# Two-layer attention network: both halves of layer 0's bias in one product for half of the keys, the two heads' maxima at the two ends of a unit, products of ones ahead of the first work

## What is computed

```python
# layer 0: all tokens see all tokens, with a relative bias per head
q, k, v = heads(x @ Wq + bq), heads(x @ Wk + bk), heads(x @ Wv + bv)
attn = q @ k.T / sqrt(64)
attn += rel_bias_h[:, :, :, :, None] + rel_bias_w[:, :, :, None, :]
out = softmax(attn) @ v
y = out @ Wp + bp
# layer 1: 7 x 7 neighbourhood attention, no bias, weights qkv_w and out_w
```

## Time and profile before

| | |
|---|---|
| time, median of 3 runs | 3215.44 us (3212.84 to 3217.96) |
| the profiled execution's own time | 3214.5 us |
| its span, first to last instruction | 3212.7 us |
| PE busy | 3144.4 us |
| DVE busy | 1703.3 us |
| ACT busy | 1225.6 us |
| POOL busy | 1084.7 us |

### The profile page before, as it was taken

One profiled execution on the slowest core, in us unless ns is written; L12 is line 12 of the kernel. 1 busy time (PEld: TensorE's weight loads), 2 busy tenths in 40 slices (PEclk: granted clock), 3 DMA queues, 4 the chain that ended last, 5 costly groups with the idle time before them and its releaser, 6 DMA issues.

```text
span 3212.7 us, 48955 instructions
## 1 busy us (share of the span) xinstructions
PE 3144.4 (98%) x20428; PEld 2349.5 (73%) x20428; DVE 1703.3 (53%) x1889; ACT 1225.6 (38%) x1397; POOL 1084.7 (34%) x618
## 2 busy tenths in 40 slices
PE   8999999999999999999999999999999999999999
PEld 6875658887787656888778766688777866668876
DVE  4447745446435774543734577444463457744434
ACT  2345542124234654213423465321342355532132
POOL 0037770025003786002400477600330057750042
PEclk9999999999999999999999999999999999999999
DMA  3211013114421101311432100221153111031113
GB/s 124 93 35 26 20 49 115 40 54 130 139 95 27 25 20 50 114 40 61 159 126 72 34 21 18 84 90 40 59 174 108 66 37 24 14 111 59 40 34 115
DMA packets 170520, 220.39 MB, mean 69 GB/s; under 512 B 113856, under 2 KB 126400, under 8 KB 170304
## 3 DMA queue, kind: packets, MB, share of 16 engines
q1 hardware_dynamic: 168768, 215.68, 21.4%
q10 hardware_dynamic: 1536, 1.57, 0.2%
HBM read 141.70 MB, written 50.33 MB: 60 GB/s over the span
## 4 chain that ended last, share of the span: by engine, by line
PE 89%; issue 4%; ACT 3%; POOL 2%; DVE 1%; DMA 0%; SPq 0%; ACTq 0%; POOLq 0%
PE score L1157 15%; PE score L1158 14%; PE score L1159 14%; PE lot L1314 13%; PE score L1279 10%; PE lot L1229 5%; PE lot L1232 3%; PE score L1286 3%; PE score L1292 2%; PE lot L1331 2%; POOL acc L568 2%; PE lot L1262 2%; ACT prob L748 1%; PE lot L1200 1%; PE lot L1157 1%
## 5 line engine op out<-in xcount | busy, mean ns | idle before, releaser
L568 POOL TENSOR_TENSOR acc<-acc,prob 128x1024 f32<-128x1024 f32 x288 | 712.9, 2475 | 208.1 <-ACT prob L748 180.9
L748 ACT ACTIVATE prob<-score 128x1024 f32<-128x1024 f32 (+3 forms) x576 | 517.6, 910 | 416.6 <-PE score L1292 292.6
L889 DVE TENSOR_REDUCE max_part<-lot 128x1 f32<-128x512 f32 x640 | 411.3, 685 | 156.3 <-PE lot L1232 156.3
L1157 PE MATMUL score<-a_hi,w_hi 128*128 128x512 f32 x1152 | 458.9, 398 | 12.9 <-DVE q_lo L1002 5.1
L1314 PE MATMUL lot<-prob,v 128*64 128x512 f32 (+4 forms) x2496 | 462.2, 513 | 5.3 <-ACT o_raw L647 3.7
L1158 PE MATMUL score<-a_lo,w_hi 128*128 128x512 f32 x1152 | 450.7, 391 | 0.0
L1159 PE MATMUL score<-a_hi,w_lo 128*128 128x512 f32 x1152 | 450.0, 391 | 0.0
L568 POOL TENSOR_TENSOR acc<-prob 128x1024 f32<-128x1024 f32 x48 | 120.1, 2502 | 833.6 <-ACT prob L748 833.6
L1157 PE MATMUL score<-w_hi,a_hi 128*128 128x256 f32 x1152 | 336.1, 292 | 0.0
L1314 PEld LDWEIGHTS lot<-prob,v 128*64 128x64 f32 x2496 | 165.6, 137 | 232.0 <-issue 193.0
L1158 PE MATMUL score<-w_lo,a_hi 128*128 128x256 f32 x1152 | 325.5, 283 | 0.0
(11 more groups left out here) (112 smaller groups left out, 5370.2 us busy)
## 6 DMA issues: line engine op xcount, KB each, us to landing
raw<-weights SPq DMA_DIRECT2D x96, 768.0 KB, 4.4
g_mem<-g SPq DMA_DIRECT2D x24, 1024.0 KB, 4.7
xin<-x_t SPq DMA_DIRECT2D x24, 512.0 KB, 6.4
xr<-x_t SPq DMA_DIRECT2D x24, 512.0 KB, 5.2
x_mem<-xr SPq DMA_DIRECT2D x24, 512.0 KB, 6.6
xr<-x_mem SPq DMA_DIRECT2D x24, 512.0 KB, 5.4
y_t<-xr SPq DMA_DIRECT2D x24, 512.0 KB, 6.9
recip<-recip SPq DMA_DIRECT2D x368, 32.0 KB, 1.9
```

What stands on the lines that cost most here:

```text
L568: nc.gpsimd.tensor_tensor(acc[:, :, a:b], with_, now, ALU.add).then_inc(added, 1)
L748: nc.scalar.activation(prob[:, ug % P_SLOTS, :, 0:b - a], score[:, u % 2, :, 0:b - a], ACT.Exp, scale=SCALE).then_inc(prob_ok, 1)
L889: nc.vector.reduce_max(max_part[:, t, part, h:h + 1], lot[:, (2 * n + h) % 3, :], AX.X)\
L1157: nc.tensor.matmul(out, w[0], a[0], start=first, stop=False)
```

## The change

In layer 0 the tokens of the normalised input are put in another order: the 16 left columns of the image first (all 32 rows), then the 16 right ones. Keys and values keep that order; the queries are put back in image order when q is copied from PSUM (ACT, and DVE in two instructions instead of one). `onehot` now differs between the layers, so it is loaded in each phase (512 KB) and cast by DVE at `j == 3`. A key tile is then 8 image rows by 16 columns, so it needs 16 rows of the row part (of which it uses 8) and 16 of the column part.

For the key tiles 4 to 7 (from unit 6 in pair 0 and unit 4 in the others, and from unit 12 in the second half) the passes with `b_hi` and `b_lo` become one pass: SP copies the needed 32 rows of both side by side into `packed[0]` or `packed[1]` (64 rows for each head; `pack`, 12 DMAs for each half of a pair, SBUF to SBUF), and `key_block` takes the place of `onehot`. `packed[0]` and `max_wide0` lie where weight chunk 10 was loaded early, so that chunk is loaded during the last pair.

The maxima ahead of a unit are no longer a block before the scores. Head 0's two products are issued beside head 1's first two score products and head 1's two beside head 0's last two, and DVE waits for each head by itself (`half_mm`).

At the program's start PE multiplies six times ones by ones (128x128 by 512, fp32), and the order of the first normalisation's steps on DVE and PE is changed.

```diff
+BLOCK = SIDE // 2
+PACKED_FROM = ([6, 12], [4, 12])
...
+    packed = [m.put("packed0", [128, 2, HALF], F32R, at=slot_at[0]),
+              m.put("packed1", [128, 2, HALF], F32R, at=one + 40 * KB)]
+    max_wide0 = m.put("max_wide0", [128, 4, 256], F32R, at=slot_at[0] + 8 * KB)
...
+                    sp.wait_ge(pack_in[1], packed_no(f, p - 3))
...
+            def pack(f, p, h):
+                s = SET_OF[0][p]
+                sp.wait_ge(b_lo_ok, f // 2 * PAIRS + p + 1)
+                if p:
+                    sp.wait_ge(score_ok, unit_no(f, p - 1, (h + 1) * QT - 1))
+                else:
+                    sp.wait_ge(v_mm, (f + 1) * VN)
+                cols = slice(h * HALF, (h + 1) * HALF)
+                to = packed[h][:, :, :].bitcast(F32)
+                for e, part in enumerate((b_hi[s], b_lo[s])):
+                    for head in range(2):
+                        a, b = 64 * head, 64 * head + BLOCK * e
+                        for n in range(2):
+                            rows = part[a + BLOCK * n:a + BLOCK * n + BLOCK, cols].bitcast(F32)
+                            sp.dma_start(to[b:b + BLOCK, n, :], rows).then_inc(pack_in[h], 16)
+                        columns = part[a + SIDE:a + SIDE + BLOCK, cols].bitcast(F32)
+                        sp.dma_start(to[b + SIDE:b + SIDE + BLOCK, :, :],
+                                     columns.unsqueeze(1).to_broadcast([BLOCK, 2, HALF]))\
+                            .then_inc(pack_in[h], 16)
+            def load_onehot(f):
+                sp.dma_start(onehot_raw[:, :], onehot_src[f % 2]).then_inc(onehot_in, 16)
...
-                weights(f, 10)
+                    weights(f, 10)
+                else:
+                    pack(f, 0, 0)
+                    pack(f, 0, 1)
...
+                        sp.wait_ge(pack_in[1], packed_no(f, LAST - 1))
                         weights(f, 9)
+                    if p:
+                        pack(f, p, 1)
+                    if p == LAST:
+                        sp.wait_ge(score_ok, unit_no(f, LAST, QT - 1))
+                        weights(f, 10)
                     spread(f, p, 0)
+                    if p < LAST:
+                        pack(f, p + 1, 0)
...
+                if f + 1 < PHASES:
+                    load_onehot(f + 1)
...
+                        if j < CT:
+                            dst, src = by_columns(dst), in_blocks(src)
...
-                src = xr[:, i, :] if f % 2 else xin[:, i, :]
-                nc.vector.tensor_scalar(xin[:, i, :], src, group_mv[:, i, 0:1],
+                if f % 2:
+                    dst, src = xin[:, i, :], xr[:, i, :]
+                else:
+                    dst, src = in_blocks(x_norm[:, i, :]), by_columns(xin[:, i, :])
...
+                    dve.wait_ge(half_mm, 2 * n + h + 1)
...
                 if i == 2:
                     aggregate(0, 0)
+                    group_means(0, 0)
                 if i == 3:
-                    group_means(0, 0)
+                    group_variances(0, 0)
+                if i == 4:
+                    norm(0, 0)
+                    norm(0, 1)
+                    input_lo(0, 0)
             aggregate(0, 1)
-            group_variances(0, 0)
-            norm(0, 0)
-            norm(0, 1)
-            input_lo(0, 0)
-            group_means(0, 1)
             norm(0, 2)
             input_lo(0, 1)
             input_lo(0, 2)
+            group_means(0, 1)
             group_variances(0, 1)
...
+                            views = [(dst[:, b], src[:, b], hi[:, b]) for b in range(2)]
+                        for dst, src, hi in views:
+                            last = nc.vector.scalar_tensor_tensor(dst, src, bqk[:, j:j + 1], hi, ALU.add,
+                                                                  ALU.subtract)
+                        last.then_inc(qk_lo_ok, 1)
...
+                    if j == 3:
+                        dve.wait_ge(onehot_in, 16 * (f + 1))
+                        nc.vector.tensor_copy(onehot[:, :], onehot_raw[:, :]).then_inc(onehot_ok, 1)
...
-            def head_maximum(f, n, sums_before):
+            def head_pass(f, n, h, e):
                 p, k = n // (2 * QT) + 1, n % (2 * QT)
-                n += f // 2 * LAST * 2 * QT
-                banks_free(sums_before)
+                no = 2 * (n + f // 2 * LAST * 2 * QT) + h
+                if e == 0:
+                    if h == 0:
+                        maximum_ready(f, p, k)
+                    if no > 2:
+                        pe.wait_ge(half_max_ok, no - 2)
+                last = maximum_pass(no % 3, f, p, k, h, e)
+                if e:
+                    last.then_inc(half_mm, 1)
+                    halves_issued[0] = no + 1
+            def head_maximum(f, n):
+                banks_free()
                 pe.wait_ge(max_ok, maxima_issued[0])
-                if n:
-                    pe.wait_ge(half_max_ok, 2 * n - 1)
-                maximum_product((2 * n % 3, (2 * n + 1) % 3), f, p, k)
-                halves_issued[0] = 2 * n + 2
+                for e in range(2):
+                    for h in range(2):
+                        head_pass(f, n, h, e)
...
-            def scores(f, p, u):
+            def scores(f, p, u, n=None):
                 layer, s, slot = f % 2, SET_OF[f % 2][p], u % 2
                 t, a, b = unit_at(layer, u)
                 keys = slice(t * 128, (t + 1) * 128)
                 ug = units_before(f, p) + u
+                half = u // QT
+                is_packed = layer == 0 and t >= QT // 2 and u >= PACKED_FROM[p > 0][half]
+                passes = 4 if layer or is_packed else 5
+                def score_pass(k, h):
+                    w = (k_hi, k_hi, k_lo, None, None)[k]
+                    x = (q_hi, q_lo, q_hi, b_hi[s], b_lo[s])[k]
+                    if k < 3:
+                        w, x = w[rows_of(h), p, keys], x[rows_of(h), p, a:b]
+                    elif is_packed:
+                        w, x = key_block[rows_of(h), t % 2, :], packed[half][rows_of(h), int(t % 4 < 2), :]
+                    else:
+                        w, x = onehot[rows_of(h), keys], x[rows_of(h), a:b]
+                    return nc.tensor.matmul(score[:, slot, h, 0:b - a], w, x,
+                                            start=(k == 0), stop=(k == passes - 1))
+                def bias_ready(k):
+                    if is_packed and u in PACKED_FROM[p > 0] and k == 3:
+                        pe.wait_ge(pack_in[half], packed_no(f, p))
+                    if u == 0 and k == 3:
+                        pe.wait_ge(shifted, pair_no(f, p))
+                        if layer == 0:
+                            pe.wait_ge(b_hi_ok, f // 2 * PAIRS + p + 1)
+                    if u == 0 and k == 4:
+                        pe.wait_ge(b_lo_ok, f // 2 * PAIRS + p + 1)
                 if p == 0 and u < 2:
                     pe.wait_ge(v_ok, (f + 1) * VN)
                 elif ug >= 2:
                     pe.wait_ge(prob_ok, ug - 1)
-                for k, (w, x) in enumerate(((k_hi, q_hi), (k_hi, q_lo), (k_lo, q_hi))):
-                    for h in range(2):
-                        nc.tensor.matmul(score[:, slot, h, 0:b - a], w[rows_of(h), p, keys],
-                                         x[rows_of(h), p, a:b], start=(k == 0), stop=False)
-                if u == 0:
-                    pe.wait_ge(shifted, pair_no(f, p))
-                    if layer == 0:
-                        pe.wait_ge(b_hi_ok, f // 2 * PAIRS + p + 1)
-                for h in range(2):
-                    last = nc.tensor.matmul(score[:, slot, h, 0:b - a], onehot[rows_of(h), keys],
-                                            b_hi[s][rows_of(h), a:b], start=False, stop=(layer == 1))
-                if layer == 0:
-                    if u == 0:
-                        pe.wait_ge(b_lo_ok, f // 2 * PAIRS + p + 1)
-                    for h in range(2):
-                        last = nc.tensor.matmul(score[:, slot, h, 0:b - a], onehot[rows_of(h), keys],
-                                                b_lo[s][rows_of(h), a:b], start=False, stop=True)
-                last.then_inc(score_ok, 1)
+                if n is None:
+                    for k in range(passes):
+                        bias_ready(k)
+                        for h in range(2):
+                            last = score_pass(k, h)
+                    last.then_inc(score_ok, 1)
+                    return
+                banks_free(int(u in (2, 10)))
+                pe.wait_ge(max_ok, maxima_issued[0])
+                for k in range(passes + 2):
+                    if k < 2:
+                        head_pass(f, n, 0, k)
+                    else:
+                        last = score_pass(k - 2, 0)
+                    if k == passes + 1:
+                        last.then_inc(score_ok, 1)
+                    if k < passes:
+                        bias_ready(k)
+                        score_pass(k, 1)
+                    else:
```

(17 more changed lines are left out.)

119 lines of the change are left out of this document (70 added, 49 removed).

## The result

The changed kernel takes 3188.18 us (median of 4 runs, 3184.02 to 3189.43), the kernel before in the same comparison 3214.14 us (4 runs, 3212.64 to 3217.96). The ratio is 0.9915, 95% interval 0.9903 to 0.9927: 26.0 us faster. The profiled execution of the changed kernel took 3189.31 us with a span of 3187.5.

The account below looks back on a forecast made before the run. PE was taken as the bound, busy 3144 of 3213 us. Gains of 25.8 + 1.9 (packing), 3 (maxima) and 2.5 (start), less 0.8 (small additions), made 32.4 us: 3182 from 3214.5, range 3168 to 3198.

Parts of the forecast that it names:

- the signs named: Included middle pair 42.6 to 42.8 us, last pair within 0.5 us of before, unit 13 waiting about 0.6 us for ACT.
- 28 slots a phase: Layer-0 attention: of 46 packed units a phase, 28 give back a 0.23 us PE slot, 25.8 us in all.
- DVE needs 1.29 of 1.38 us, so it keeps up: Packed units with a maximum: DVE's work for two heads fits the shortened unit, so PE is not held.
- The margin of less than 0.1 us: Packed units: ACT's exponential fits about 1.3 us into 1.38; missing by 0.1 us repeatedly would cost 6 us.
- (a) Units 12 and 13: Pairs 1 to 4: ACT's chain makes shorter units wait, so both slots are lost, 8 a phase.
- (c) The last pair: POOL's unbroken additions hold the sums; 8 slots a phase lost, 0.3 us kept.
- Of the 8.1 us I keep 3: PE's waits for DVE's row maxima, twice a phase in pair 0: 3 us gained, bounds 0 and 8.1.
- The copies: SP's copies to packed, covered by 5 us before the first packed unit in pairs after pair 0; cost nothing.
- The start: Program start: earlier normalising and products of ones gain 2.5 us, bounds -1 and 6.
- Rival 2: ACT or DVE bounds packed units, half the 112 slots go: gain about 15 us, 3199; chance 0.07 for 6 to 14.
- Rivals 3 and 4: 3: freed slots waited for elsewhere, 3210 to 3220, chance 0.05. 4: first-half copies land late, kernel slower, chance 0.06.
- rival 1: Gain over 45 us: ACT chain at units 12 and 13 gives way, all maxima waits go, start gives 6; chance 0.06.

Follow-up runs that it names:

- the five-pass kernel: Changed kernel with its copies, waits and order kept, but five passes in every unit of layer 0; 3209.24 us, ratio 0.9979.
- the block order: Changed kernel with a unit's maximum as one block of four products ahead of its scores, as before the change; 3191.55 us, ratio 0.9927.
- shorter maxima: Changed kernel with DVE reading 384 of 512 columns for each head's maximum of pairs 1 to 5, part of the maximum left out; 3183.05 us, ratio 0.9893.
- the second trace: Profiled execution of the unaltered changed kernel run once more, 3182.3 us without any stretch at half rate; median 3186.39 us, ratio 0.991.
- the added products: Changed kernel with first bias, onehot cast and layer-1 rounding moved later, plus four more products of ones behind the first shift averages; 3172.94 us, ratio 0.9867.
- the first trace: First profiled execution of the unaltered changed kernel, with three stretches at half rate; 3189.31 us, span 3187.5.
- the kernel with the later first bias: Changed kernel with ACT's first bias copy of pair p+2 behind the output copy at unit 12 instead of behind unit 10; 3183.55 us, ratio 0.9903.
- the later layer-1 rounding: Changed kernel with ACT rounding the weight chunk of layer 1's last pairs behind unit 7 instead of unit 6; 3179.84 us, ratio 0.9896.

## Why the prediction was right, and where it was off

The forecast was 3182, the median 3188.18, a gain of 26 us where the sum said 32.4, in the range and on the right side. An execution without a stretch at half rate took 3182.3, but the sum did not know of these. Of the signs named, these came: PE waits 1.00 us for POOL at the last pair's first sums, 0.62 for ACT at unit 13, 2.7 for the maxima in all, and the first projection stands at 19.39. A middle pair of 42.85 us and a last pair 0.7 us shorter lie just outside what was named. Step by step:

1. **"28 slots a phase ... 25.8 us, plus ... 1.9 us"**, 27.7 us for packing. Measured by the five-pass kernel, with packing added last: 21.1 (26.7 when it is added first, see the block order). This is the term that was mis-sized, and the sentence that failed is "DVE needs 1.29 of 1.38 us, so it keeps up". It keeps up on average, but not behind a reciprocal of 1.75 us: then it reads seven heads without a break at 0.67 us each, and the weight loads wait. With shorter maxima a middle pair gains 1.75 instead of 1.25. That the waits of the weight loads (7.0 us) come near the shortfall (6.6) is in part chance: in the second trace they are 5.7 with the same pairs. By the marks, of the 1.65 us that are short in a phase 1.0 is at units 2 to 5 of pairs 1 to 4, behind the reciprocals, 0.45 at the end of pair 0, 0.2 at units 14 and 15 of pair 4, where PE waits for ACT, and about 0.4 is spread over the other stretches; the last pair gives 0.4 back. So the failed sentence is shown to cost 4 of the 6.6 us, and up to 6 with the end of pair 0, where the weight loads wait for DVE too. The margin of less than 0.1 us that the prediction feared for was ACT's; that one held. PE's waits for `prob` rose by 5.7 us, over half of it at unit 13 (0.35 to 0.62), where it was expected.
2. **(a) Units 12 and 13.** Right: the wait of 0.35 us became 0.62, the groups behind unit 13 gain 0.00, and moving ACT's rounding gives 0.2 to 0.3 us of it back.
3. **(c) The last pair.** The bound was right (POOL, 1.00 us of wait at the first sums), the size too low: 0.69 us from the last group of pair 4's values on, instead of 0.3. It is packing alone. The prediction counted only what the second half's sums would let go.
4. **"Of the 8.1 us I keep 3"**, less 0.8 for the split of q's rest. Measured for all that is not packing, without packing beside it: 7.4 us in attention, 4.0 of it at the end of pair 0 and 0.2 at units 2 to 5 of each pair. The waits for maxima fell to 2.7, and to 1.8 in the second trace, so 5.4 to 6.3 us came back: the waits did not return at the next bank. By the block order, the new order of the maxima is worth only some 0.4 us a phase next to packing, all of it in pair 0.
5. **The copies: nothing.** Right; 4 us of cover instead of 5. There are 576 copies a run, not 288, which is the number for the first halves alone.
6. **The cast of onehot: nothing.** Wrong, 2.8 us. It stands on DVE ahead of `g` of pair 1 (q's products with the table of the relative bias), and PE waits 0.7 us at L1294. The prediction asked what covers the cast, not what stands behind it on DVE.
7. **The start: 2.5 us.** Measured 4.35 at the first mark and 0.7 lost to the cast on the way, so 5.1. The mechanism named, the group mean ahead of POOL's w_lo, is right. What was missed is that the ones decide whether it happens, because they halve the time of the 14 small products. The clock at the first projection was not what they changed: behind 5.83 us of idle PE ran at half rate, 0.43 us a product, and with the added products at the full rate it started no earlier. The Trainium skill (TensorE: Matmul & The Clock Gate, The two states you'll see) lets an idle PE fall back to half rate, and by that rule the prediction kept only 0 to 2 us; the trace agrees with the rule, and not with that consequence. The reading that the clock rose some 5 us after dense work began was made from 28.94 on and left out a row: PE had been at work since 23.40, with averages between the projections. Before the change:

```profile
26.10 2.98 PE L1169 MATMUL lot<-shift,group 128*128 128x1 f32 x14
```

   The ones ended at 8.69 all the same, near the 9 us forecast: a right result on an incomplete reading. How much of the 5.1 us is this execution's own stays open, since the first mark varies.
8. **Not in the sum: stretches at half rate.** 1.66 us each, two more than in the trace of before. The sum was made against one execution that had one.

The errors cancel by half: packing -6.6, cast -2.8, half rate -3.3, start +2.6, the maxima and small additions +5.2, less 1.5 for the single wait of phase 0 and 0.6 of remains. 32.4 - 6.6 - 2.8 - 3.3 + 2.6 + 5.2 - 1.5 - 0.6 = 25.4, against 25.2 measured. That the median fell so well into the range owes something to this luck, above all to the maxima and the start, which gave more than was counted.

Rival 2 (ACT or DVE becomes the bound in the packed units) was real for DVE, at 6.6 us or less and not 13. Rivals 3 and 4 did not occur; rival 1's ACT chain gave way only when it was moved.

## What to carry over

A mean margin of a tenth of a microsecond for an engine that must keep up is none: look for the longest instruction that stands in its list just ahead of the tight stretch, and count from there. Read the waits of PE's weight loads beside those of its products, since a wait can show there alone. For each small addition to an engine's list, ask what stands behind it and who waits for that, not only what covers it. To tell a kernel's gain from an execution's, compare distances between marks that both traces share, since whole spans of one kernel differed here by 7 us.

## What the runs showed of the hardware

- The same kernel with the same wait of 1.26 us of PE ran the 24 products behind it in 4.05 us once and in 2.38 another time. All traces together have 31 such stretches. The longest wait of PE in the few us ahead of them was 1.26 us in 13, 1.36 in 7, about 0.4 in 8 (at the end of a layer-1 phase, where the small averages follow), and 0.94, 1.32 and 1.94 in the other three. In the second trace none of these waits was followed by one. What decides it stays open.
- In phase 0 of the first trace DVE's normalisation took 2.83 us beside POOL's additions, in the second no such wait of PE followed. DVE (line, then what it waited for):

```profile
260.72 2.83 DVE L1022 TENSOR_TENSOR o_raw<-o_raw,recip 128x512 f32<-128x512 f32 x1 [2.50 <-DMA recip<-recip]
```

The maximum behind it was late, and PE waited 0.92 us at 264.20. The same instruction lasts 0.69 us in the second trace and in the kernel with the later first bias, with POOL adding there too; it was slow again in the kernels with the maxima as a block (2.77) and the later layer-1 rounding (2.68). That the two engines shared a port there was only argued.
